# Convolution read straight from the accumulation bank, and the second norm with its projections as a chain of their own

## The chip, the cores and the metric

The kernel runs on one core of one Trainium2 chip. The metric is the device time of one execution in microseconds (us); lower is better. All of the work sits in one launch: five engines (TensorE, here PE; VectorE, DVE; ScalarE, ACT; GpSimd, POOL; and SyncE, SP, which only issues transfers) each run a program of their own and meet at semaphores.

## The reference, cut to what matters

The model is a two-layer decoder over 64 sequences of 128 tokens with 256 features. The change touches only the first layer, whose three sublayers are, for each sequence:

```
x = x + mamba(layernorm(x))            # in_proj, causal conv of 4 taps, scan over time, gate by silu(z), out_proj
x = x + cross_attention(layernorm(x), ctx, ctx, mask)    # q from x, k and v from ctx, 16 heads of 16
x = x + moe(layernorm(x))              # shared expert + top 2 of 16 experts

xc = conv(x_ssm, conv_w, padding=(3, 0)) + conv_b        # per channel: 4 taps over time
x_ssm = silu(xc)
y = scan(dt, A, B, C, x_ssm) + D * x_ssm
y = rmsnorm(y) * silu(z)
```

The routed experts and the second layer come in later phases of the same launch and are the same in both kernels.

## The kernel before

The launch has three phases. Phase 1 does the first layer's three sublayers for all 64 sequences, except for the routed experts, whose rows it scatters; phase 2 runs the experts; phase 3 does the second layer. One sequence fills the 128 partitions with its 128 tokens (or, transposed, with 128 features).

Phase 1 is a software pipeline. The work on a sequence is cut into chains, named by a letter: M (first norm, the step sizes dt and their running sums), V (input projections, convolution, gate), N (scan as masked products, output projection, residual x1), Y (keys and values from the context), X (cross-attention), F (third norm, router, shared expert). Body n of the loop runs M and V for sequence n, N for n-1, Y and X for n-2 and F for n-3. `program` unrolls the first and last bodies, which hold fewer chains, and loops over the full ones. Each chain is a Python generator that yields a step's name before it issues the step, and `weave` runs the generators in the order of the table `ORDER`, one line for each engine. So `Vcv` is step "cv" of chain V, and what stands in the table is the very order in each engine's queue. Every engine takes its queue strictly in order; `done` waits for a signal of this sequence, `was` waits until the previous sequence no longer needs a buffer. Nearly all buffers exist once.

The steps that the text below speaks of:

- POOL: `d0` to `d3` (differences of running sums, L618), `m3` (a mask product, L622), M's `sp` (the softplus series, 13 small operations, L594 to L610), `yg` (gate product, L625), `rms`, `ln1` to `ln3` (four tiny operations each, L582 to L585), F's `sc` (two indirect scatters).
- DVE: `cv` to `cv3` (the convolution: four taps, each in four pieces of 128x128; the first at L817, the others at L819), `m0` to `m2` of N (mask products, L847), `y0` and `y1` (L852), `xs2` (L826), `xdt` (L836, L837), `gz` (L841), `cb` (L830), `x1` (L861), `m0` to `m3` of X (row maxima of scores, L769 and L772), `ho` (heads out, L784 to the second residual at L880), F's `r`, `top` and `slot` (router, L889 to L912), `xo` (L920).
- PE: `bc`, `ip1`, `z` (input projections), `CB`, `xsT`, `v0` to `v3` (scan products, L1488), `yT`, `pr` (output projection), Y's `cT`, `k`, `v`; X's `ln2n`, `q`, `s0`, `s2` (scores), `t0` to `t3` (transposes of probabilities, L1425), `pv` (L1434), `OT`; F's `r`, `rk`, `gu`, `hT`, `dn`.
- ACT: copies out of the banks, `g`/`e` (absolute value and exponential), the softmax, `cth` and `tz` (tanh), `xp`.

The accumulation banks (PSUM) are Q[0] to Q[7]. Q[1] holds in turn, for chain V, `bc`, `ip1`, `CB`, `xsT` and `z`. In the kernel before, ACT's `xp` copies `ip1` to the padded SBUF tile `xpad`, and the convolution reads that.

Of the kernel before, what the change touches and what calls it, by code (L numbers as in the profile page):

```python
# [89 lines left out]
def two_layers(nc, x_d, ctx_d, m0_d, m1_d, w_in, conv_w, conv_b, a_log, d_p, dt_bias, norm_w, w_out,  # L90
# [8 lines left out]
    with ExitStack() as ctx:  # L99
# [105 lines left out]
        xpad = part(IC * (T + NCONV - 1)).rearrange("p (c t) -> p c t", c=IC)  # L205
# [73 lines left out]
        signals("V", "DVE", "conv xs2 cbm xdt gz")  # L279
        signals("V", "PE", "bc ip1 CB xsT z")  # L280
        signals("V", "ACT", "bcT xpad conv_th tz")
# [3 lines left out]
        signals("Y", "DVE", "k0c")  # L285
        signals("Y", "PE", "ctxTps k0 v0")
        signals("Y", "ACT", "ctxT v0c")
        signals("X", "DVE", "ln2_var S0max:4 x2")
        signals("X", "PE", "ln2_Tps q0 S0:4 PT0ps:4 PV0:2")
        signals("X", "ACT", "ln2_xn mrow ln2_T q0c P0:4 PT0s:4 OT0")  # L290
        signals("X", "POOL", "x1r ln2_rstd")
# [30 lines left out]
        links = {"M_DVE": 3, "V_DVE": 3, "X_DVE": 5, "F_DVE": 15, "A_DVE": 5, "C_DVE": 1, "K_DVE": 2, "T_DVE": 7, "M_POOL": 13, "N_POOL": 1, "X_POOL": 3,  # L322
# [71 lines left out]
        def _(sp):  # L394
# [74 lines left out]
            program(sp, "SP", 1, (("M", M, 0), ("N", N, 1), ("Y", Y, 2), ("X", X, 2), ("F", F, 3)))  # L469
# [61 lines left out]
        def _(pool):  # L531
# [6 lines left out]
            g.memset(xpad, 0.0)  # L538
# [92 lines left out]
            def X(b):  # L631
# [5 lines left out]
                centre("ln2", mvX, b, "X_POOL")  # L637
# [11 lines left out]
            program(pool, "POOL", 1, (("M", M, 0), ("N", N, 1), ("X", X, 2), ("F", F, 3)))  # L649
# [68 lines left out]
        def _(dve):  # L718
# [1102 lines left out]
```

How the kernel before makes its waits and increments, by code:

```python
        def done(eng, name, b, k=1):  # L124
            eng.wait_ge(SEM[name], at(name, b, k))
# [1 line left out]
        def was(eng, name, b, k=1):  # L127
            if not isinstance(b, int) or b > 0:
                eng.wait_ge(SEM[name], at(name, b, k) - PER[name])
# [202 lines left out]
        def link(eng, name, b, ins, bare=False):  # L333
            steps[name] += 1
            assert steps[name] <= links[name], name
            ins.then_inc(SEM[f"link_{name}"], 1)
            eng.wait_ge(SEM[f"link_{name}"], at(f"link_{name}", b, steps[name]))
            if bare:
                eng.sem_inc(SEM[f"passed_{eng.engine.name}"], 1)
# [28 lines left out]
        def met(eng, me, k):  # L369
            eng.sem_inc(SEM[f"phase_{me}"], 1)
            for other in ("PE", "DVE", "ACT", "POOL"):
                if other != me:
                    eng.wait_ge(SEM[f"phase_{other}"], k)
# [18 lines left out]
        @block.sync  # L393
# [67 lines left out]
            def F(b):  # L461
                yield "m"
                done(sp, "slot", b)
                tell(sp.dma_start(rows(slot_d, b), meta[:, :]), "meta_out", 16)
                yield "o"
                done(sp, "xo", b)
                tell(sp.dma_start(rows(x2_d, b), xo), "xo_out", 16)
            program(sp, "SP", 1, (("M", M, 0), ("N", N, 1), ("Y", Y, 2), ("X", X, 2), ("F", F, 3)))
            sp.wait_ge(SEM["plan"], 1)
            sp.dma_start(routed_d[SPARE:SPARE + P, :], zero).then_inc(SEM["tails"], 16)
            zeros_behind(sp, range(NE // 2))
            sp.wait_ge(SEM["scattered"], at("scattered", NB, 0))
```

## Time and profile before

| | |
|---|---|
| median of 3 runs | 4827.91 us (4826.06 to 4829.62) |
| the profiled execution | 4827.89 us, its span 4826.3 us |
| PE busy | 4224.3 us, 88% of the span |
| DVE, ACT, POOL busy | 3368.1 us (70%), 2909.1 us (60%), 2734.9 us (57%) |
| mean granted clock of TensorE | 0.923 of full speed |

A busy time is the sum of an engine's instructions over the span. Phase 1 takes about the first 2516 us of it. In phase 1 no engine is busy all the time, so the busy shares do not say what bounds it; the order of the queues and the waits between them do.

### The profile page before, as it was taken

The page shows a single profiled execution, that of the slowest core. Times are in us where ns is not written, and L with a number is a line of the kernel's source. Part 1 is how long each engine was busy: PE and PEld are TensorE (multiplying, and loading weights), DVE is VectorE, ACT ScalarE, POOL GpSimd, SP SyncE. Part 2 cuts the span into 40 slices and gives each one's busy share as a digit, 9 for nine tenths or more (in the row PEclk, how much of TensorE's full clock was granted, in tenths as well). Part 3 has the DMA queues.
Part 4 walks back from the last instruction along what each step waited for, and adds up shares of the span by engine and source line. Part 5 has one row for each costly group of instructions (what it writes and reads, how often), then busy time and mean ns, then how long its engine had stood idle before and what let it go on. Part 6 is the DMA issues. An engine that isn't in the chain of part 4 may idle for free.

```text
span 4826.3 us, 119218 instructions
## 1 busy us (share of the span) xinstructions
PE 4224.3 (88%) x33430; PEld 3093.7 (64%) x33431; DVE 3368.1 (70%) x8668; ACT 2909.1 (60%) x7030; POOL 2734.9 (57%) x4093
## 2 busy tenths in 40 slices
PE   3788888888888888888869979999999999999998
PEld 2666666666666666666647756666666666666665
DVE  2776677666776667766745547777777777777776
ACT  2666666666666666666634436666666666666564
POOL 3666666666666666666622235555555555555554
PEclk9888888888888888888979989999999999999998
DMA  5222222222222222222214411111111111111110
GB/s 155 72 82 90 74 74 74 89 83 74 74 78 92 75 74 74 83 88 75 74 59 145 144 39 31 30 31 31 31 29 31 30 31 31 31 31 31 31 31 18
DMA packets 215885, 304.09 MB, mean 63 GB/s; under 512 B 56608, under 2 KB 167456, under 8 KB 215840
## 3 DMA queue, kind: packets, MB, share of 16 engines
q1 hardware_dynamic: 188864, 240.33, 16.0%
q0 software_dynamic: 19200, 52.45, 3.3%
q10 hardware_dynamic: 7776, 10.75, 0.7%
q8 instruction: 23, 0.38, 0.0%
q14 instruction: 22, 0.18, 0.0%
HBM read 239.19 MB, written 64.23 MB: 63 GB/s over the span
## 4 chain that ended last, share of the span: by engine, by line
PE 51%; POOL 20%; issue 17%; DVE 6%; ACT 2%; POOLq 1%; SPq 1%; DMA 0%; DVEq 0%; ACTq 0%
PE Q L1397 14%; PE Q L1402 8%; POOL arena L618 7%; PE Q L1390 6%; PE Q L1488 4%; PE Q L1425 3%; PE Q L1735 3%; PE Q L1768 3%; PE Q L1589 3%; PE Q L1434 2%; POOL arena L625 2%; PE Q L1601 2%; POOL arena L605 1%; PE Q L1419 1%; POOL arena L606 1%
## 5 line engine op out<-in xcount | busy, mean ns | idle before, releaser
L1402 PE MATMUL Q<-ident,arena 128*128 128x128 f32 x4768 | 801.5, 291 | 148.7 <-ACT arena L1145 35.3
L1402 PEld LDWEIGHTS Q<-ident,arena 128*128 128x128 f32 x4768 | 557.0, 145 | 388.2 <-issue 123.7
L1397 PE MATMUL Q<-Wkvl,arena 128*128 128x512 f32 x1024 | 500.3, 601 | 0.0
L618 POOL TENSOR_TENSOR arena<-arena 128x1024 f32<-128x1024 f32 x256 | 479.4, 1889 | 7.2 <-DMA arena<-cum_rows 7.2
L682 POOL TENSOR_TENSOR l<-l,half_pow 128x8 f32<-128x8 f32 x192 | 318.5, 1659 | 233.2 <-DVE l L1025 231.3
L707 POOL TENSOR_TENSOR arena<-arena,part_of 128x512 f32<-128x512 f32 x256 | 263.7, 1041 | 190.8 <-DVE part_of L1063 190.4
L1488 PE MATMUL Q<-arena 128*16 128x128 f32 x4096 | 223.6, 339 | 169.1 <-DVE arena L847 167.9
L769 DVE TENSOR_REDUCE mx<-Q 128x4 f32<-128x512 f32 x512 | 343.9, 681 | 10.2 <-PE Q L1419 5.5
L1425 PEld LDWEIGHTS Q<-ident,arena 128*128 128x128 f32 x2048 | 244.2, 148 | 116.5 <-issue 84.9
L1425 PE MATMUL Q<-ident,arena 128*128 128x128 f32 x2048 | 314.0, 288 | 1.3 <-ACT arena L1155 0.4
L1155 ACT ACTIVATE arena<-Q,mx 128x128 f32<-128x128 f32 x1024 | 281.8, 372 | 0.7 <-DVE mx L769 0.5
L1419 PE MATMUL Q<-arena 32*128 32x128 f32 x4096 | 278.7, 274 | 0.0
L1162 ACT ACTIVATE arena<-Q 128x512 f32<-128x512 f32 x384 | 222.0, 597 | 83.2 <-PE Q L1425 79.1
L1488 PEld LDWEIGHTS Q<-arena 128*16 128x16 f32 x4096 | 129.4, 107 | 222.2 <-DVE arena L847 169.0
L1202 ACT ACTIVATE arena<-arena 128x1024 f32<-128x1024 f32 x256 | 268.4, 1048 | 0.1
L1199 ACT ACTIVATE arena<-arena 128x1024 f32<-128x1024 f32 x256 | 268.3, 1048 | 0.0
L1419 PEld LDWEIGHTS Q<-arena 32*128 32x128 f32 x4096 | 261.4, 188 | 3.6
L1361 ACT ACTIVATE arena<-Q,mxl 128x256 f32<-128x256 f32 x512 | 235.4, 472 | 45.0 <-DVE mxl L1058 37.6
L1390 PEld LDWEIGHTS Q<-arena,Win 128*128 128x128 f32 x1536 | 235.8, 235 | 33.5 <-issue 29.2
L1434 PE MATMUL Q<-arena 128*17 128x128 f32 x4096 | 208.1, 276 | 41.4 <-ACT arena L1162 41.4
L1390 PE MATMUL Q<-arena,Win 128*128 128x128 f32 x1536 | 236.9, 315 | 3.1 <-ACT arena L1184 2.2
L1397 PEld LDWEIGHTS Q<-Wkvl,arena 128*128 128x128 f32 x1024 | 170.3, 191 | 104.2 <-issue 104.0
(310 smaller groups left out, 10753.3 us busy)
## 6 DMA issues: line engine op xcount, KB each, us to landing
arena<-cum_rows SPq DMA_DIRECT2D x256, 512.0 KB, 6.1
arena<-routed_rows SPq DMA_DIRECT2D x144, 128.0 KB, 2.1
expert_rows<-arena POOLq DMA_DIRECT2D x144, 128.0 KB, 2.0
arena<-in_x_dram SPq DMA_DIRECT2D x128, 128.0 KB, 4.4
arena<-in_ctx_dram SPq DMA_DIRECT2D x128, 128.0 KB
x_rows<-arena SPq DMA_DIRECT2D x128, 128.0 KB, 1.7
arena<-x_rows SPq DMA_DIRECT2D x128, 128.0 KB, 2.3
out_dram<-arena SPq DMA_DIRECT2D x64, 128.0 KB, 1.7
```

The source lines that it names most:

```text
L618: tell(g.tensor_tensor(E8[j], E8[j], cums[:, 8 * j:8 * j + 8].unsqueeze(2).broadcast_to([P, 8, T]), ALU.subtract), "diff")
L682: link(pool, c, b, g.tensor_tensor(l2[:, k, :], l2[:, k, :], half_pow[:, :], ALU.pow), bare=True)
L769: largest = v.tensor_reduce(mx[:, 4 * j:4 * j + 4], pj, AX.X, ALU.max, negate=True)
L1155: last = s_.activation(S[:, j, g, :], banks[j][:, g * T:(g + 1) * T], ACT.Exp, bias=mx[:, 4 * j + g:4 * j + g + 1])
L1202: tell(s_.activation(Ew[j], Ew[j], ACT.Exp, scale=-1.0), "E")
L1390: last = mm(out, lhs(c), rhs(c), start=c == 0, stop=c == n - 1)
L1397: last = mm(out, lhs(c), rhs(c), start=c == 0, stop=c == n - 1)
L1402: last = nc.tensor.transpose(out[:, c * P:(c + 1) * P], src[:, c * P:(c + 1) * P], ident[:, :])
L1419: last = mm(banks[j][:, g * T:(g + 1) * T], QT[r, g, :], KT[r, g // 2, :], start=False, stop=g == NG - 1)
L1425: last = nc.tensor.transpose(bank[:, g * T:(g + 1) * T], S[:, j, g, :], ident[:, :])
L1434: last = mm(bank[32 * (h % 4):32 * (h % 4) + AW + 1, h // 4 * T:(h // 4 + 1) * T], V[:, h, :], PT[:, j, g, :], start=True, stop=True)
L1488: last = mm(Q[3 + j // 2][32 * (i % 4):32 * (i % 4) + HP, (h // 4 % 4) * T:(h // 4 % 4 + 1) * T], xdt[:, h * HP:(h + 1) * HP], E8[j][:, i, :],
```

## The change

- The convolution reads the bank Q[1] directly, tap by tap, with the time shift in the slices instead of in a padded tile. The first tap becomes a multiply-add with two scalars per partition (`tensor_scalar`), the other three stay as they were, with the bank as their source. `xpad`, its memset and ACT's copy `xp` go away. `CB` can no longer use Q[1] beside the convolution, so `CB` and `cb` move behind `z` and `gz`.
- The second norm, its transposes and the query projection move from chain X to chain Y (and from banks Q[5], Q[6] to Q[2]). Y now stands for sequence n-2, X for n-3 and F for n-4: five sequences in flight, 68 bodies instead of 67.
- Chain N swaps the banks of `yT` and `pr`.
- The table `ORDER` for phase 1 is rewritten on all five engines.

```diff
     1: {
         "SP": """
-            Ncb0 Ncb1 Ncb2 Yc Xm Mx Ncb3 Nx Mco Fm Fo
+            Ncb0 Ncb1 Xm Ncb2 Ncb3 Nx Mx Yc Fm Mco Fo
         "POOL": """
-            Nd0 Nd1 Nd2 Xx1r Fln3 Xln2 Mln1 Nd3 Msp Nm3 Fsc Nyg Nrms
+            Nd0 Nd1 Nd2 Fln3 Nd3 Mln1 Fsc Nm3 Msp Yx1r Yln2 Nyg Nrms
...
             def V(b):
                 J = lambda ins, bare=False: link(dve, "V_DVE", b, ins, bare)
-                yield "cv"
-                done(dve, "xpad", b)
-                for k in range(NCONV):
-                    if k:
-                        yield f"cv{k}"
+
+                for late in range(NCONV):
+                    yield f"cv{late}"
+                    if late == 0:
+                        done(dve, "ip1", b)
                     for c in range(IC):
-                        src, wk = xpad[:, c, k:k + T], convw[:, c, k:k + 1]
-                        out = xc[:, c * T:(c + 1) * T]
-                        if k == 0:
-                            last = v.scalar_tensor_tensor(out, src, wk, convb[:, c:c + 1].broadcast_to([P, T]), ALU.mult, ALU.add)
+                        src, wk = Q[1][:, c * T:(c + 1) * T - late], convw[:, c, NCONV - 1 - late:NCONV - late]
+                        out = xc[:, c * T + late:(c + 1) * T]
+                        if late == 0:
+                            last = v.tensor_scalar(out, src, wk, convb[:, c:c + 1], ALU.mult, ALU.add)
                         else:
                             last = v.scalar_tensor_tensor(out, src, wk, out, ALU.mult, ALU.add)
...
-                yield "xp"
-                done(act, "ip1", b)
-                tell(s_.activation(xpad[:, :, NCONV - 1:], cut(Q[1][:, :], IC), ACT.Copy), "xpad")
...
-            program(pe, "PE", 1, (("M", M, 0), ("V", V, 0), ("N", N, 1), ("Y", Y, 2), ("X", X, 2), ("F", F, 3)))
+            program(pe, "PE", 1, (("M", M, 0), ("V", V, 0), ("N", N, 1), ("Y", Y, 2), ("X", X, 3), ("F", F, 4)))
```

The first place is DVE in the middle and second half of a full body. In the rows a line number is that of the kernel they belong to, and rows that only set registers are left out. Before:

```order
L847 TENSOR_TENSOR arena<-arena 128x1024
L769 TENSOR_REDUCE mx<-Q 128x4
L920 TENSOR_TENSOR arena<-Q,arena 128x256
L817 SCALAR_TENSOR_TENSOR arena<-arena,convw,convb 128x128 x4
L819 SCALAR_TENSOR_TENSOR arena<-arena,convw 128x128 x12
L852 TENSOR_TENSOR arena<-Q,arena 128x256
L826 SCALAR_TENSOR_TENSOR arena<-arena 128x512
```

In the changed kernel the same place reads:

```order
L815 TENSOR_SCALAR arena<-Q,convw,convb 128x128 x4
L817 SCALAR_TENSOR_TENSOR arena<-Q,convw,arena 128x127 x4
L817 SCALAR_TENSOR_TENSOR arena<-Q,convw,arena 128x126 x4
L920 TENSOR_TENSOR arena<-Q,arena 128x256
L782 RECIPROCAL rc<-Q 128x16
L783 TENSOR_TENSOR arena<-Q,rc 128x256
L880 TENSOR_TENSOR arena<-arena 128x256
L817 SCALAR_TENSOR_TENSOR arena<-Q,convw,arena 128x125 x4
L852 TENSOR_TENSOR arena<-Q,arena 128x256
L824 SCALAR_TENSOR_TENSOR arena<-arena 128x512
```

The convolution's source is now Q, and `xo` (L920) and `ho` (L782 to L880) stand between its third and its last tap; before, `ho` stood at the start of the body, behind `x1`.

The second place is PE at the end of a full body, behind the transposes of y. Before:

```order
L1434 MATMUL Q<-arena 17x128 x8
L1402 MATMUL Q<-ident,arena 128x128 x4
L1434 MATMUL Q<-arena 17x128 x4
L1397 MATMUL Q<-Win,arena 128x512 x2
L1397 MATMUL Q<-Wout,arena 128x256 x4
```

And in the changed kernel:

```order
L1388 MATMUL Q<-arena,Wq 128x128 x4
L1400 MATMUL Q<-ident,arena 128x128 x4
L1395 MATMUL Q<-Win,arena 128x512
L1400 MATMUL Q<-ident,arena 128x128 x2
L1395 MATMUL Q<-Win,arena 128x512
L1388 MATMUL Q<-arena,Wk 128x128 x4
L1388 MATMUL Q<-Wv,arena 128x256 x2
L1471 MATMUL Q<-arena 128x128
L1395 MATMUL Q<-Wout,arena 128x256 x4
```

Now the query, key and value projections (Wq, Wk, Wv) and `CB` (L1471) stand around `z` (Win) and ahead of the output projection (Wout); `pv` (17x128) has moved to the middle of the body.

The third place is DVE at the start of a full body of the changed kernel, up to the router's maximum:

```order
L752 BN_STATS stF<-arena 128x6
L767 TENSOR_REDUCE mx<-Q 128x4
L770 TENSOR_TENSOR arena<-Q,mx 128x512
L752 BN_STATS stM<-arena 128x6
L752 BN_STATS stX<-arena 128x6
L847 TENSOR_TENSOR arena<-arena 128x1024
L889 TENSOR_REDUCE rt<-Q 128x1
```

Two pairs of L767 and L770 and two L847 stand there. Before, the scores stood behind the router.

## Rows read from the trace of the kernel before

**Rows 1.** Timeline of POOL: start, length, the gate product in three bodies

```profile
105.25 1.27 POOL L625 TENSOR_TENSOR arena<-arena 128x512 f32<-128x512 f32 x1 [3.97 <-DVE arena L852]
211.17 1.28 POOL L625 TENSOR_TENSOR arena<-arena 128x512 f32<-128x512 f32 x1 [3.25 <-DVE arena L852]
...
2425.67 1.27 POOL L625 TENSOR_TENSOR arena<-arena 128x512 f32<-128x512 f32 x1 [3.15 <-DVE arena L852]
```

**Rows 2.** Stretches of phase 1: from:to, length, busy (instructions) of each engine, clock, DMA

```profile
800.00:1100.00 300.00, 249.80 (x2064) 190.25 (x2062) 208.69 (x561) 196.42 (x424) 191.00 (x289) 0.87 0.24 79
...
1011.60:1018.60 7.00, 6.71 (x28) 6.14 (x29) 2.73 (x16) 3.72 (x11) 3.39 (x7) 0.52 0.00 0
```

**Rows 3.** Waits over 40 bodies (500 to 2000 us): total, times, longest

```profile
POOL arena L594 <- DVE arena L804: 244.7, 40, 6.1
...
PE Q L1488 <- DVE arena L847: 105.3, 40, 2.6
```

**Rows 4.** Timeline of one body, DVE: start, length, instruction

```profile
1006.66 0.25 DVE L784 RECIPROCAL rc<-Q 128x16 f32<-128x16 f32 x1
1008.15 0.43 DVE L754 BATCH_NORM_STATS2 stF<-arena 128x6 f32<-128x256 f32 x1
1009.57 1.22 DVE L847 TENSOR_TENSOR arena<-arena 128x1024 f32<-128x1024 f32 x1
1010.72 0.42 DVE L754 BATCH_NORM_STATS2 stM<-arena 128x6 f32<-128x256 f32 x1
1014.97 0.17 DVE L889 TENSOR_REDUCE rt<-Q 128x1 f32<-128x16 f32 x1 [3.50 <-PE Q L1390]
1018.25 0.17 DVE L902 TENSOR_TENSOR selb<-sel 128x16 bf16<-128x16 f32 x1
1021.26 0.68 DVE L769 TENSOR_REDUCE mx<-Q 128x4 f32<-128x512 f32 x1
1022.58 0.68 DVE L769 TENSOR_REDUCE mx<-Q 128x4 f32<-128x512 f32 x1
1028.55 3.24 DVE L817 SCALAR_TENSOR_TENSOR arena<-arena,convw,convb 128x128 f32<-128x128 f32 x4
1031.83 3.56 DVE L819 SCALAR_TENSOR_TENSOR arena<-arena,convw 128x128 f32<-128x128 f32 x12
```

**Rows 5.** Timeline of PE in the same body, and two rows of the last bodies

```profile
1004.05 1.89 PE L1397 MATMUL Q<-Wout,arena 128*128 128x256 f32 x8
1017.41 1.65 PE L1390 MATMUL Q<-arena,Win 128*128 128x128 f32 x8
1020.65 1.98 PE L1397 MATMUL Q<-Wsgu,arena 128*128 128x512 f32 x4
1022.47 1.95 PE L1390 MATMUL Q<-arena,Win 128*128 128x128 f32 x16
2479.09 3.78 PE L1397 MATMUL Q<-Wsgu,arena 128*128 128x512 f32 x4
2491.74 1.76 PE L1434 MATMUL Q<-arena 128*17 128x128 f32 x32
```

**Rows 6.** Single lines: count, shortest/median/longest in ns, first and last start

```profile
L817 DVE SCALAR_TENSOR_TENSOR arena<-arena,convw,convb x256: 332/340/2459, 65.6 to 2419.9; 128x128 f32<-128x128 f32 x128
L622 POOL TENSOR_TENSOR arena<-arena x64: 2361/2409/2424, 98.9 to 2453.0; 128x1024 f32<-128x1024 f32 x64
```

**Rows 7.** Timeline of DVE in the last two bodies: second residual and x2 out

```profile
2466.09 0.48 DVE L861 SCALAR_TENSOR_TENSOR arena<-Q,ss,arena 128x256 f32<-128x256 f32 x1 [5.83 <-PE Q L1397]
2495.70 0.42 DVE L880 TENSOR_TENSOR arena<-arena 128x256 f32<-128x256 f32 x1
2513.48 0.42 DVE L920 TENSOR_TENSOR arena<-Q,arena 128x256 f32<-128x256 f32 x1 [2.14 <-PE Q L1390]
```

**Rows 8.** Timeline of SP and POOL in the second body: a transfer and its user

```profile
69.33 0.36 SPq L437 DMA_DIRECT2D cum_rows<-arena  x1
...
74.90 5.60 POOL L618 TENSOR_TENSOR arena<-arena 128x1024 f32<-128x1024 f32 x3 [7.23 <-DMA arena<-cum_rows]
```

More of the change, by code:

```diff
@@ L278, in two_layers @@
         signals("M", "POOL", "ln1_rstd a")
-        signals("V", "DVE", "conv xs2 cbm xdt gz")
-        signals("V", "PE", "bc ip1 CB xsT z")
-        signals("V", "ACT", "bcT xpad conv_th tz")
+        signals("V", "DVE", "conv xs2 xdt gz cbm")
+        signals("V", "PE", "bc ip1 xsT z CB")
+        signals("V", "ACT", "bcT conv_th tz")
         signals("N", "DVE", "M:3 y2 x1")
@@ L284, in two_layers @@
             sig(n, k)
[L285 to L291, printed above, removed]
+        signals("Y", "DVE", "ln2_var k0c")
+        signals("Y", "PE", "ln2_Tps q0 ctxTps k0 v0")
+        signals("Y", "ACT", "ln2_xn ln2_T q0c ctxT v0c")
+        signals("Y", "POOL", "x1r ln2_rstd")
+        signals("X", "DVE", "S0max:4 x2")
+        signals("X", "PE", "S0:4 PT0ps:4 PV0:2")
+        signals("X", "ACT", "mrow P0:4 PT0s:4 OT0")
         signals("F", "DVE", "ln3_var rmax sel slot hh xo")
@@ L841, in V @@
                 tell(v.scalar_tensor_tensor(gz, tz, 1.0, Q[1][:, :], ALU.add, ALU.mult), "gz")
+                yield "cb"
+                done(dve, "CB", b)
+                was(dve, "M3", b)
+                tell(v.tensor_tensor(cbm, Q[1][:, 0:T], triu[:, :], ALU.mult), "cbm")
             def N(b):
@@ L1213, in N @@
                 done(act, "yTps", b)
-                tell(s_.activation(yT, cut(Q[4][:, :], IC), ACT.Copy), "yT")
+                tell(s_.activation(yT, cut(Q[3][:, :], IC), ACT.Copy), "yT")
             def Y(b):
+                yield "ln2"
+                normal("ln2", x1, xn2, mvX, b)
+                yield "ln2n"
+                copyT("ln2", Q[2], xT2, b)
+                yield "q"
+                done(act, "q0", b)
+                was(act, "S0", b, 4)
+                src = cut(Q[2][:, D:2 * D], DC)
+                dst = QT0.rearrange("p (c k) q -> p c k q", k=2)
+                for k in range(2):
+                    for c in range(DC):
+                        last = s_.activation(dst[:, c, k, :], src[:, c, :], ACT.Identity, bias=bq0s[:, c, k:k + 1], scale=par[:, k:k + 1])
+                tell(last, "q0c")
                 yield "cT"
@@ L1232, in X @@
                 tell(s_.activation(mrow[:, :], mask0i[:, :], ACT.Identity, bias=eps[:, 2:3]), "mrow")
-                yield "ln2n"
-                copyT("ln2", Q[6], xT2, b)
-                yield "q"
-                done(act, "q0", b)
-                src = cut(Q[5][:, 0:D], DC)
-                dst = QT0.rearrange("p (c k) q -> p c k q", k=2)
-                for k in range(2):
-                    for c in range(DC):
-                        last = s_.activation(dst[:, c, k, :], src[:, c, :], ACT.Identity, bias=bq0s[:, c, k:k + 1], scale=par[:, k:k + 1])
-                tell(last, "q0c")
                 yield from softmax(b, banks, S0, mx0, 0)
@@ L1452, in V @@
                 done(pe, "ln1_T", b)
-                was(pe, "gz", b)
+                was(pe, "cbm", b)
                 for k in range(2):
@@ L1474, in V @@
                 tell(last, "z")
+                yield "CB"
+                done(pe, "gz", b)
+                tell(mm(Q[1][:, 0:T], bcT[:, 0, :], bcT[:, 1, :], start=True, stop=True), "CB")
             def N(b):
```

71 lines of the change are left out of this document (32 added, 39 removed).

## The prediction

> **What bounds the kernel now.** I read the page's busy shares (which name no bound), then the stretches, the timeline of one body, the waits and the chain of waits. Phase 1 is a loop: POOL's gate product starts at 211.17 us in one body and at 2425.67 us 59 bodies later [rows 1], so a full body takes 37.53 us, and 64 sequences make about half of the time. In a steady stretch of 300 us no engine is full: PE 250, DVE 209, ACT 196 and POOL 191 us [rows 2]. That is 31.2, 26.1, 24.6 and 23.9 us of a body. So the body is as long as the chain of hand-offs that runs once round it through queues that are taken strictly in order. The waits say the same: POOL stands 6.1 us in each body for DVE's dt ratio and 3.2 us for `y1` [rows 1], PE 2.6 us for the first mask product [rows 3], DVE 3.5 us for the router's product [rows 4].
>
> Two more things lengthen a body. First, PE's clock: from 1011.6 to 1018.6 us the granted clock was 0.52, its lower level of 1.2 GHz, behind the stretch in which PE stood idle for 2.6 us [rows 2, 3]. Four matmuls of an input projection took 1.65 us there, where eight took 1.95 us at the full 2.4 GHz; two products 512 wide took 3.78 us at the low and 1.98 us at the full level [rows 5]. Second, DVE and POOL get in each other's way. The first tap of the convolution takes 0.34 us at the median, but at the most 2.46, and in each body four pieces take 3.24 us [rows 4, 6]: one of them stands for as long as POOL's mask product, 2.41 us [rows 6]. The Trainium skill, page "SBUF — State Buffer", section "Who interferes with whom", says that a VectorE instruction with two SBUF inputs and GpSimd's reads exclude each other for the whole instruction. The trace agrees: the blocked piece has the padded tile and the broadcast bias as its inputs. By that rule the new first tap, whose one tensor lies in a bank, is never blocked; if the pair of engines were in each other's way whatever the operands, the three early taps would last 2.1 us longer and outlast their cover (below) by 0.7 us, and the sum would be 4837 us.
>
> **The change part by part.**
>
> *The convolution.* The first tap now has one input, in the bank, and the others one in the bank and one in SBUF. Nothing here can be blocked by POOL like the piece of 2.46 us: the first tap's four pieces should take about 4 times 0.29, 1.15 us, as four pieces of the later taps do (12 in 3.5) [rows 4]. DVE saves 2.1 us of a body, POOL nothing. ACT saves `xp`, a copy of a full bank (about 0.6 us, as the other copies of a bank), which is not on the path. Does the bank as a source cost time? A 128x256 sum took 0.42 us with both inputs in SBUF and 0.42 us with one in a bank [rows 7], so I take nothing; the bound upward is one piece's 0.05 us, 0.8 us a body. The Trainium skill, "VectorE: DVE Perf Modes", section "Rules for kernel authors", says to copy a bank to SBUF first when many operations will read it, which speaks against this change. By that rule the copy would pay only where an instruction has a faster mode from SBUF, and the two rows show none for a form with two inputs.
>
> *The order.* I followed the new queues once round, from the end of `y1` on DVE to the same point in the next body, always taking the later of "engine free" and "input there". Durations are distances between starts in the timeline of one body; steps under 1 us that have no row of their own are read there too. The path that I find:
>
> - `y1` to `x1`: POOL's gate product 1.27 plus a hand-off 0.08; transposes 0.6; first half of `z` 0.9; context transposes 0.35; second half 0.9 (two such products 1.98 [rows 5]); key and value projections 0.95 and 0.85 (from eight matmuls in 1.95, full clock); `CB` 0.2; `pr` 1.89 [rows 5]; `x1` 0.48 and 0.3 for its waits. Sum 8.8 us. Query, key and value used to run at the low clock beside other work; here they are on the path but at full clock.
> - DVE alone: three norms' moments at 0.71 (two in 1.42), two score steps at 1.32, two mask products at 1.15 [rows 4]: 7.1 us. None of it is new work; it now lies in one queue between `x1` and the router.
> - router's maximum to `sel`: 3.45 [rows 4], plus 0.1 for a hand-off: 3.55 us.
> - PE: rank 0.2, `t0` 0.5, `bc` 1.5 at low clock, `gu` 3.2 (between 1.98 and 3.78, nearer to the low clock), `ip1` 1.95 [rows 5]: 7.35 us.
> - `hT` 0.4, `t1` 0.6, its copy on ACT 0.6, `t3` 0.5, four `pv` steps 1.8 (1.76 [rows 5]), `dn` 0.85, `OT` 0.65, with 0.1 for hand-offs: 5.5 us.
> - `ho` 1.45 (L784 to the next norm at 1008.15 [rows 4]), `cv3` 1.15, tanh 0.7, `xs2` 0.65, `y1` 0.4: 4.35 us.
>
> The sum is 36.65, with 0.05 left over in rounding 36.7 us, 0.83 us less than 37.53. What lies beside it: the first three taps (3.5 us) end 1.4 us before `dn`, so most of what DVE saves there stays hidden; if PE's part between were shorter, it would come out. POOL does its scatters, `m3` and the softplus one after another behind `slot` and ends them about 0.8 us before PE comes to `Mcum`. If that cover goes, each us there lengthens the body. The transfer of the sums now starts some 2.7 us before `y1` ends and took 5.6 us to its user [rows 8], so `d0` starts 3 us after `y1`, 1 us after `rms` lets it. POOL's three differences end at 8.7, the third norm's moments come at 9.5: hidden by 0.8. Behind POOL's late norm wait ACT's `Fln3` and PE's router, which is where a late transfer would come out.
>
> *The extra body.* 68 bodies instead of 67. The last body with F alone took 17.8 us, from the second residual to `xo`, the one with Y, X and F 29.6 [rows 7]. The new one has X and F: between the two, and I take 22. The early bodies get lighter, since X and F start later; today three early bodies take 35.3 us each (105.25 to 211.17 us) [rows 1], 6.6 us less in all, and one more such step may save between 1 and 8 us; I take 5. Together +17 us, between +10 and +28.
>
> *The sum.* 60 full bodies at -0.83 are -50 us, the extra body +17. From the profiled execution's 4827.9 us (span 4826.3 and 1.6 around it; the median of three runs is 4827.91, the same): **4795 us**.
>
> **The rivals.**
>
> *Slower: the low clock lasts longer.* Between the scores at the start and `sel` I find PE busy for some 4 of 10 us, with one gap of 2.3 us and three over 1. Today 7.0 us at the low level follow one gap of 2.6 us [rows 2, 3]. It has to come back during `gu` for my sum. If it comes back only within `ip1`, that costs up to 1.45 us more (3.4 instead of 1.95), and `gu` 0.5 more [rows 5]. The change loses as soon as a body is 0.55 us longer than my sum: 60 bodies must save at least the 17 us of the extra one, 0.28 each, and they save 0.83. At +1.3, a body of 38.0, the time is 4827.9 + 28 + 17 = 4873 us; with all of `ip1` slow (+2) it is 4915. For it speaks that `bc` and `gu` follow directly on the thin stretch; against, that PE is packed from `sel` on.
>
> *Faster: the clock holds.* The gaps are each shorter than today's. Then `bc` saves 0.55 and `gu` 1.4: a body of 34.75 and 4678 us. Against it speaks how little PE does in that stretch.
>
> *Faster: the convolution's 2.1 us come out in full*, since DVE is what is waited for in the second half: 60 times 2.1 is 126, plus 17: 4719 us. For it: the convolution stands between `ip1` and `y0` in the chain of today. Against it: my layout hides it behind `pv` and `dn`.
>
> *No change:* the path is the same length with other names, a body of 37.1 to 37.4, and 4819 to 4837 us.
>
> **How the numbers follow.** My forecast, 4770 to 4817 us: 0.35. Slower by the clock: 0.31. Faster by the clock 0.08, by the convolution 0.14. No change 0.12. Faster by over 0.2% (10 us, about what a measurement of this kernel can tell from no change) is 0.35 + 0.08 + 0.14 = 0.57, same 0.12, slower 0.31. The range reaches down past the convolution's case, to 4705, and up to 4880, past the middle of the slow case; it leaves out the far end of the slow case and the held clock, about 2 in 10.
>
> **What would show it.** In the changed kernel's profile: gate products 36.7 us apart; all 16 pieces of the convolution at about 0.35 us with no long one; the granted clock about 0.85 in the loop, low from before the router until within `gu`; DVE without a gap from `x1` to the router's maximum; POOL idle some 6 us before the scatters. My sum is wrong if `ip1` shows the low clock (slower), if DVE waits long before `xo` and `ho` (then the convolution is hidden, as I say) or does not wait there at all (then it counts), or if POOL's `d0` waits for the transfer well past 3 us after `y1`.

## The result, and the profile after

The changed kernel takes 4860.7 us, the median of 4 runs (4859.21 to 4863.27), beside 4826.99 us for the kernel before. The ratio is 1.0073, with a 95% interval of 1.0055 to 1.009: it is slower by 34 us, where 4795 us and a gain were forecast. The profiled execution took 4860.3 us, its span 4858.7 us.

Timeline of POOL in the changed kernel, the gate product in four bodies (start, length, instruction, idle time before it and what ended that):

```profile
100.98 1.27 POOL L623 TENSOR_TENSOR arena<-arena 128x512 f32<-128x512 f32 x1 [4.76 <-DVE arena L852]
207.33 1.27 POOL L623 TENSOR_TENSOR arena<-arena 128x512 f32<-128x512 f32 x1 [1.75 <-DVE arena L852]
2425.09 1.27 POOL L623 TENSOR_TENSOR arena<-arena 128x512 f32<-128x512 f32 x1 [2.16 <-DVE arena L852]
2460.29 1.27 POOL L623 TENSOR_TENSOR arena<-arena 128x512 f32<-128x512 f32 x1
```

Between the second and the third row lie 59 bodies: 37.59 us each, beside 37.53 before [rows 1] (one of them takes 41.4 us, the others average 37.5). The loop gained nothing, where 0.83 us a body were forecast. It did not lose the 34 us either: the gate product at 2425.09 stands where that of before stood (2425.67 us). Almost all of the loss is behind it.

Timeline of DVE behind the loop: the last residual x1 (L861), xo (L920) and x2 (L880) of the last bodies, and the first instruction of phase 2 (L943):

```profile
2469.51 0.48 DVE L861 SCALAR_TENSOR_TENSOR arena<-Q,ss,arena 128x256 f32<-128x256 f32 x1 [1.30 <-PE Q L1395]
...
2491.93 0.42 DVE L880 TENSOR_TENSOR arena<-arena 128x256 f32<-128x256 f32 x1
...
2529.57 0.43 DVE L880 TENSOR_TENSOR arena<-arena 128x256 f32<-128x256 f32 x1
...
2548.90 0.42 DVE L920 TENSOR_TENSOR arena<-Q,arena 128x256 f32<-128x256 f32 x1 [3.33 <-PE Q L1388]
2551.37 0.27 DVE L943 MEMSET arena<- 128x256 f32 x1 [2.04 <-DMA x_rows<-arena]
```

From the last x1 to the last xo it is 79.4 us, in three bodies of 22.4, 37.6 and 19.3. Before it was 47.4 us, in two of 29.6 and 17.8 [rows 7]. That is 32 us, the whole loss within 2. (From the gate product at 2425.09 to the last x1 it is 4.0 us more than before; the start of phase 1 is 3.8 us shorter and the later phases are 3 us shorter.) So two things have to be explained: why a body is not shorter, and why the last ones are so long.

Stretches of the changed kernel (from:to, length, busy time of PE, weight load, DVE, ACT, POOL, granted clock, DMA), the second one the 14 us behind PE's longest wait in a body:

```profile
800.00:1100.00 300.00, 258.04 (x2062) 191.13 (x2054) 193.84 (x560) 193.23 (x416) 183.49 (x288) 0.82 0.24 79
893.80:907.80 14.00, 13.32 (x81) 9.34 (x82) 10.33 (x35) 9.24 (x20) 6.55 (x8) 0.51 0.08 25
```

DVE is busy for 15 us less of 300 [rows 2]: the convolution's saving is real. POOL is busy for 7.5 less, but that is the order's work: with the new convolution in the old order (`conv_alone` below) the same stretch has DVE at 194.59 and POOL still at 191.05 us. The clock went from 0.87 to 0.82. It now stays at its lower level of 1.2 GHz for 14 us at a time, where it was 7.0. It did not double a body's time at that level, though: before, most bodies had a second low stretch of 3.4 us, which the prediction did not read (granted 0.51 from 841.1 to 844.5 us and 0.50 from 861.6 to 868.4). As a share of time it went from about a quarter to about a third (worked out from 0.87 and 0.82, with 0.5 for the lower level).

The waits over 40 bodies (500 to 2000 us; total, times, longest):

```profile
POOL routed_rows L644 <- DVE meta L912: 267.9, 40, 6.7
...
PE Q L1400 <- ACT arena L1145: 162.6, 116, 2.9
...
POOL arena L633 <- DVE arena L880: 39.1, 36, 1.2
```

POOL stands 6.7 us before the scatters, as forecast. In the last row POOL's `x1r` (L633) waits for x2 (L880), about 1 us a body. The wait itself is not new. The kernel before has it too:

```profile
POOL arena L635 <- DVE arena L880: 27.9, 40, 0.7
```

But there it held up nothing: in one body of that kernel `x1r` runs from 857.86 to 858.59 us, and the moments of the second norm (`mvX`) are ready only at 859.38. In the body of the changed kernel below they are ready at 821.19 us, 20 us before POOL comes to them. What is new is that `x1r` has a finished norm behind it. The price shows in one full body, on POOL, ACT and PE:

```profile
839.84 0.25 POOL L608 TENSOR_TENSOR arena<-arena,Aneg 128x32 f32<-128x32 f32 x1 [0.18 <-POOL arena L607]
840.15 0.41 PE L1444 MATMUL Q<-arena,triu 128*128 128x32 f32 x2
841.15 0.73 POOL L633 TENSOR_TENSOR arena<-arena,bv0b 128x256 f32<-128x256 f32 x1 [1.05 <-DVE arena L880]
841.83 0.19 POOL L580 TENSOR_TENSOR mvX<-mvX,eps 128x1 f32<-128x1 f32 x1
...
843.76 0.60 ACT L1145 ACTIVATE arena<-arena,mvX 128x256 f32<-128x256 f32 x1 [0.86 <-POOL mvX L583]
...
844.41 0.87 PE L1400 MATMUL Q<-ident,arena 128*128 128x128 f32 x6 [1.31 <-ACT arena L1145]
845.32 1.16 PE L1388 MATMUL Q<-arena,Wq 128*128 128x128 f32 x8
846.32 0.60 PE L1400 MATMUL Q<-ident,arena 128*128 128x128 f32 x4
```

The second norm's four tiny operations (L580 to L583) stand behind `x1r` in POOL's queue. So the norm comes late, PE stands 1.31 us at its transposes, and behind them in PE's queue are the query projection (Wq), `yT`, `z` and the output projection, that is x1. The gate product ends at 845.36 us (844.09 and 1.27), but its transposes `yT` start only at 846.32, behind the query projection.

### The profile page after: what moved, and what is told of

Its sections match the earlier page's. It is cut to its first block, busy times and chain, and to the rows that moved or that the text cites. A ratio compares the mean times of both kernels' runs of the same rounds, so it can differ in the third digit from the quotient of the medians.

```text
span 4858.7 us, 118978 instructions
## 1 busy us (share of the span) xinstructions
PE 4291.8 (88%) x33430; PEld 3114.9 (64%) x33431; DVE 3260.6 (67%) x8668; ACT 2883.9 (59%) x6966; POOL 2670.3 (55%) x4092
## 4 chain that ended last, share of the span: by engine, by line
PE 68%; DVE 10%; issue 9%; POOL 5%; ACT 5%; DMA 1%; DVEq 1%; SPq 1%; POOLq 0%; ACTq 0%
PE Q L1395 20%; PE Q L1388 14%; PE Q L1400 11%; PE Q L1423 4%; PE Q L1432 3%; PE Q L1735 3%; PE Q L1768 3%; PE Q L1589 3%; DVE mx L767 2%; ACT arena L1225 2%; PE Q L1601 2%; PE Q L1417 1%; ACT arena L1145 1%; DVE arena L847 1%; PE Q L1487 1%
## 5 line engine op out<-in xcount | busy, mean ns | idle before, releaser
L1400 PEld LDWEIGHTS Q<-ident,arena 128*128 128x128 f32 x4768 | 561.0, 147 | 661.3 <-ACT arena L1145 299.8
L644 POOL DMA_INDIRECT routed_rows<-arena,meta x128 | 150.7, 1178 | 461.8 <-DVE meta L912 439.1
L767 DVE TENSOR_REDUCE mx<-Q 128x4 f32<-128x512 f32 x512 | 350.1, 684 | 9.0 <-PE Q L1417 4.3
L1417 PE MATMUL Q<-arena 32*128 32x128 f32 x4096 | 331.9, 309 | 0.0
L1423 PE MATMUL Q<-ident,arena 128*128 128x128 f32 x2048 | 313.3, 295 | 17.8 <-ACT arena L1162 16.0
L1417 PEld LDWEIGHTS Q<-arena 32*128 32x128 f32 x4096 | 315.0, 221 | 7.2
L1423 PEld LDWEIGHTS Q<-ident,arena 128*128 128x128 f32 x2048 | 251.8, 151 | 100.5 <-issue 66.0
L1388 PEld LDWEIGHTS Q<-arena,Win 128*128 128x128 f32 x1536 | 246.3, 243 | 46.0 <-issue 43.1
L1388 PE MATMUL Q<-arena,Win 128*128 128x128 f32 x1536 | 247.1, 323 | 1.9 <-ACT arena L1184 1.9
L847 DVE TENSOR_TENSOR arena<-arena 128x1024 f32<-128x1024 f32 x192 | 229.6, 1223 | 1.9 <-issue 0.4
```

Source lines behind the costliest of these rows:

```text
L767: largest = v.tensor_reduce(mx[:, 4 * j:4 * j + 4], pj, AX.X, ALU.max, negate=True)
L847: tell(v.tensor_tensor(E8[j], E8[j], cbm.unsqueeze(1).broadcast_to([P, 8, T]), ALU.mult), "M")
L1388: last = mm(out, lhs(c), rhs(c), start=c == 0, stop=c == n - 1)
L1400: last = nc.tensor.transpose(out[:, c * P:(c + 1) * P], src[:, c * P:(c + 1) * P], ident[:, :])
L1417: last = mm(banks[j][:, g * T:(g + 1) * T], QT[r, g, :], KT[r, g // 2, :], start=False, stop=g == NG - 1)
L1423: last = nc.tensor.transpose(bank[:, g * T:(g + 1) * T], S[:, j, g, :], ident[:, :])
```

## The experiments

The theory after the result: `x1r` of a sequence waits for x2 of the one before, now made in the same body; that delays the second norm a little in every body and a lot in the last ones. The rival: the longer low clock eats the loop's gain. A second rival: the convolution's place. Each kernel was timed beside the kernel before on the same chip. Ratios are to that kernel, intervals 95%. Not all kernels had the same chip, so differences between two experiments are given by their ratios, too. Of a queue the diffs show the part that changes, "..." stands for the rest.

**The convolution alone.** Kernel `conv_alone`: the kernel before with the new convolution and `CB` behind `gz`, everything else in its old order.

```diff
-... Fxo Vcv Vcv1 Vcv2 Vcv3 Ny0 Vxs2 Ny1 Vcb Vxdt Vgz Nx1 Xho
+... Fxo Vcv0 Vcv1 Vcv2 Vcv3 Ny0 Vxs2 Ny1 Vxdt Vgz Vcb Nx1 Xho
```

> The kernel before with the convolution alone changed: it reads the bank, the copy to the padded tile is gone, CB and cb stand behind z and gz; chains, stages and the rest of the order as before. Theory A (the gain of the convolution is real and was lost to the order, the clock and the extra body): DVE is on the path from ip1 to y1 there, the blocked piece of 2.46 us goes, and a body gets 1.2 to 2.1 us shorter: 4700 to 4755 us. Rival B (the convolution brings nothing wherever it stands): within 10 us of 4827. Rival C (the bank held longer costs, since CB now waits for gz): slower, over 4840.

4832.43 us, ratio 1.0015 (1.0006 to 1.0024). Timeline of DVE at the place of [rows 4]:

```profile
1029.00 1.35 DVE L815 TENSOR_SCALAR arena<-Q,convw,convb 128x128 f32<-128x128 f32 x4
1030.39 3.42 DVE L817 SCALAR_TENSOR_TENSOR arena<-Q,convw,arena 128x127 f32<-128x127 f32 x12
1035.05 0.42 DVE L852 TENSOR_TENSOR arena<-Q,arena 128x256 f32<-128x256 f32 x1 [1.25 <-PE Q L1399]
1036.90 0.69 DVE L824 SCALAR_TENSOR_TENSOR arena<-arena 128x512 f32<-128x512 f32 x1 [1.42 <-ACT arena L1187]
```

The gain expected under theory A (4700 to 4755 us) did not come. The convolution takes 4.8 us instead of 6.8, and DVE then waits 1.25 us for PE, where it did not wait before, and 1.42 us for the tanh, where it was 0.36 to 0.50. Even in the old order its 2 us were not on the path: the rival by which they come out in full is refuted there. The edit moves `CB`, too, so a small gain of the one and a small loss of the other are not told apart. The granted clock in the stretch from 800 to 1100 us rose to 0.94, from 0.87, and brought nothing either.

**The convolution made dearer.** Kernel `conv_twice`: the changed kernel with the first tap computed twice.

> The changed kernel with the convolution's first tap computed twice (four more pieces of 128x128, 1.4 us of DVE a body). The prediction put the first three taps beside pv and dn with 1.4 us to spare; the profile after shows DVE waiting 0.7 us between the third tap and xo. If the first three taps are hidden, the body grows by only what exceeds that spare, 0.7 us at most: 4860 to 4905 us. If DVE's convolution lies on the path, it grows by the whole 1.4 us: 4945 us or so.

4867.12 us, ratio 1.0071 (1.0057 to 1.0085), against 1.0073 for the changed kernel. 1.4 us more of DVE for each sequence, some 88 us in all, cost about 6 us by the medians and nothing by the ratios. The first three taps are hidden, as the prediction's layout had it. In the loop DVE no longer waits for PE before `xo`, where it waited 0.7 us in the changed kernel, so this cover, forecast at 1.4 us, is used up.

**The bias as a tensor.** Kernel `bias_tensor`:

```diff
-v.tensor_scalar(out, src, wk, convb[:, c:c + 1], ALU.mult, ALU.add)
+v.scalar_tensor_tensor(out, src, wk, convb[:, c:c + 1].broadcast_to([P, T]), ALU.mult, ALU.add)
```

> The changed kernel with the first tap as the two-operand form it had before, source in the bank and the broadcast bias from SBUF, so that one operand more comes from SBUF. If only two inputs in SBUF get in POOL's way, no piece of the first tap is long: all near 0.34 us and the time is that of the changed kernel within 0.2%. If POOL's traffic blocks any instruction that reads a tensor from SBUF twice over its output, some pieces last over 1 us while POOL's mask product runs.

4861.95 us, ratio 1.007 (1.0055 to 1.0085). Single lines (count, shortest/median/longest in ns), first of this kernel, then of the changed one:

```profile
L815 DVE SCALAR_TENSOR_TENSOR arena<-Q,convw,convb x256: 339/343/353, 64.2 to 2415.5; 128x128 f32<-128x128 f32 x128
```

```profile
L815 DVE TENSOR_SCALAR arena<-Q,convw,convb x256: 401/404/414, 64.2 to 2414.7; 128x128 f32<-128x128 f32 x128
```

The very form that stood for up to 2459 ns before [rows 6] is never blocked once its source is a bank. All 256 pieces ran beside some instruction of POOL, but only 25 of them beside its mask product. `conv_alone` makes this firm: 316 pieces of its later taps, with one input in the bank and one in SBUF, ran beside the mask product, and the longest took 352 ns. What blocked the first tap was the second input from SBUF. The Trainium skill, "SBUF — State Buffer", section "Who interferes with whom", states that a VectorE instruction with at most one input in SBUF, outside the modes that use both ports, does not contend with GpSimd; the trace agrees in all of these pieces.

**The second norm ahead of x1r.** Kernel `norm_first`:

```diff
-... Fsc Nm3 Msp Yx1r Yln2 Nyg Nrms
+... Fsc Nm3 Msp Yln2 Yx1r Nyg Nrms
```

> The changed kernel with one swap on GpSimd: the second norm's scale ahead of x1r, so that it no longer waits for the previous sequence's second residual. Theory A (x1r's wait for x2 holds back the whole query and key chain): in the last bodies the chain starts 2 to 13 us earlier, and in a full body 0.3 to 1.0 us comes off: 4790 to 4840 us. Rival B (the wait is covered in full bodies): only the last bodies gain, 4850 to 4858.

4839.73 us, ratio 1.0025 (1.0015 to 1.0035): 21 us below the changed kernel. Bodies of 36.7 and of 37.5 us alternate in stretches (the profiled execution, 4821.86 us, was the fastest of nine). Gate product and x1 in a short body:

```profile
870.17 1.27 POOL L623 TENSOR_TENSOR arena<-arena 128x512 f32<-128x512 f32 x1 [2.05 <-DVE arena L852]
...
878.57 0.48 DVE L861 SCALAR_TENSOR_TENSOR arena<-Q,ss,arena 128x256 f32<-128x256 f32 x1 [1.49 <-PE Q L1395]
```

From the start of the gate product to the end of x1 it is 8.9 us, where three of four bodies of the changed kernel take 9.9: the 1.0 us by which the short bodies are shorter. The wait for x2 is part of the loss, in the loop and behind it. But PE now stands before the running sums for POOL's softplus series: 48.0 us in the 40 bodies from 500 to 2000 us, against 7.7 in the changed kernel.

**Filler matmuls.** `fill_before` puts 12 small matmuls of the identity, into columns that nobody reads, ahead of `v0` in the kernel before. `fill_after` puts 25 a body into the changed kernel, where PE stands idle between the scores and `sel`.

> The kernel before with 12 such extra matmuls a body ahead of the first scan product, where TensorE stands idle for 2.6 us. If the low clock of 7.0 us a body costs there too: a body gets 1 to 1.7 us shorter, 4725 to 4770 us. If its projections there are hidden behind DVE's router: within 15 us of 4827.

> The changed kernel with 25 extra small matmuls a body (128x128 by 64 columns, into a free part of bank Q[0]; their results are not used) put where TensorE waits: 12 ahead of the third norm's transposes, 3, 6 and 4 ahead of the router, the first norm's transposes and the ranks. Theory A (the low clock, 14.7 us of a body, costs the time): the granted clock stays at 1.00, gu takes 1.98 us instead of 3.42 and bc 0.95 instead of 1.9, a body gets 1.5 to 2.5 us shorter, 4705 to 4770 us. Rival B (the path there is DVE's and ACT's, the clock only fills waits): 4850 to 4870. Rival C (the extra matmuls stand in the way): slower than 4880.

`fill_before`: 4804.55 us, ratio 0.995 (0.9934 to 0.9967). `fill_after`: 4873.68 us, ratio 1.0097 (1.0079 to 1.0115). Both missed their forecast gains (4725 to 4770 and 4705 to 4770 us). The bodies of `fill_before` are 36.0 us in some stretches and 37.5 in others: in the kernel before, the low clock costs up to 1.5 us a body, not always given back. In `fill_after` the part of the body that ran at 0.51 now runs at the full level, and yet it is no faster (the two intervals overlap; its bodies take 37.55 us). Stretch, then timelines of POOL and PE in the same body (gate product at 811.53, the next at 849.08):

```profile
823.50:837.50 14.00, 13.64 (x135) 11.23 (x133) 11.82 (x39) 11.20 (x26) 6.46 (x8) 1.00 0.06 20
```

```profile
833.53 1.40 POOL L644 DMA_INDIRECT routed_rows<-arena,meta  x1 [6.82 <-DVE meta L912]
835.23 0.96 POOL L644 DMA_INDIRECT routed_rows<-arena,meta  x1 [0.30 <-issue]
836.21 2.38 POOL L620 TENSOR_TENSOR arena<-arena 128x1024 f32<-128x1024 f32 x1
838.54 0.24 POOL L592 TENSOR_TENSOR arena<-arena 128x32 f32<-128x32 f32 x1
...
844.36 0.25 POOL L608 TENSOR_TENSOR arena<-arena,Aneg 128x32 f32<-128x32 f32 x1 [0.18 <-POOL arena L607]
```

```profile
844.67 0.41 PE L1449 MATMUL Q<-arena,triu 128*128 128x32 f32 x2 [2.79 <-POOL arena L608]
```

PE finishes its part early and stands 2.79 us for the end of the softplus series, which on POOL lies behind the scatters and the fourth mask product: 11 us from the first scatter to L608. The sums start 33.1 us behind the gate product. In the body of the changed kernel shown above, the series ended at 840.09 (839.84 + 0.25) and PE, which had just finished its work before them, began the sums at 840.15, 33.7 us behind its gate product at 806.42. That is no chance of this body: in the loop the sums begin 0.05 to 0.18 us behind the end of the series, and in 8 of 54 bodies PE stands 1.9 us for it. So two paths of nearly equal length end there, PE's at the low clock and POOL's. A faster clock alone cannot pay.

**POOL's path.** `sp_first` moves the softplus series ahead of the mask product in the changed kernel; `pool_order` does it in `norm_first`.

```diff
-... Fsc Nm3 Msp ...
+... Fsc Msp Nm3 ...
```

> The changed kernel with one exchange in POOL's queue: the softplus series ahead of the fourth mask product. If POOL's series is one of two paths of equal length at the end of a body, this alone is worth little, since x1r still waits for x2 and the second norm with it: the period 37.0 to 37.5, 4825 to 4860 us. If POOL's queue alone set the end in the changed kernel, it gains as much as it did in pool_order on top of norm_first, 0.9 us a body or more: 4810 us or less.

> norm_first with the softplus series ahead of the fourth mask product on POOL. There PE waited 1.5 us a body for the series before the running sums. If POOL's work behind the router's slot (scatters, mask product, softplus) sets the end of a body, the sums come 2.4 us earlier, the last scan product then waits for the mask product, and a body is 1.0 to 1.6 us shorter: 4740 to 4780 us. If the low clock sets it, the body falls back to 37.5 or 36.7 us all the same and the time is within 10 us of norm_first (4830 to 4845).

`sp_first`: 4848.48 us, ratio 1.0032 (1.002 to 1.0044). `pool_order`: 4769.62 us, ratio 0.9877 (0.9862 to 0.9891), 36.26 us a body. Against the changed kernel the one exchange brings 12 us, the other 21, and both together 91; by the ratios 0.41%, 0.48% and 1.96%. That is how two paths of equal length look: each edit alone shortens only one of them. One rival stays: most bodies of `sp_first` and many of `norm_first` take 37.5 us, a length that bodies of other kernels have as well (see the end), so something else may hold a body there until both edits are made.

**The clock once more, with POOL's path loosened.** `pool_fill` is `pool_order` with the 25 fillers. `m3_dve` is `pool_order` with the fourth mask product on DVE (POOL's queue, then DVE's, in the diff), `m3_fill` is that with the fillers.

```diff
-... Fsc Msp Nm3 Yln2 Yx1r Nyg Nrms
+... Fsc Msp Yln2 Yx1r Nyg Nrms
-... Nm2 Msp Xm3 Fhg ...
+... Nm2 Msp Xm3 Nm3 Fhg ...
```

> pool_order with the 25 filler matmuls a body of fill_after, which held the clock except for some 4 us at the end of a body, where PE stood idle 2.8 us for the softplus series. If the fillers gained nothing in fill_after because the clock's gain was spent waiting for POOL, they gain here: 36 us a body or less, 4745 us or less, and below pool_order. If they gain nothing because they delay what they stand in front of, the time is at or above pool_order's.

> pool_order with the fourth mask product on DVE (1.2 us there, where it waited 1.9 us for the gate's tanh) instead of POOL (2.4 us). In pool_order PE no longer waited for POOL at the end of a body, so if the path there is PE's own part at the low clock, it changes little: 4755 to 4785 us. If POOL still set it, a body is 1 us or more shorter: 4710 us or less.

> m3_dve with the 25 filler matmuls a body. In pool_fill the clock was full, but x2's sum on DVE stood 2.4 us beside POOL's mask product and PE waited 1.55 us for that product. Without the product on POOL both go: if these two ate the clock's gain, a body is 34.3 to 35.5 us, 4660 to 4730 us, and below m3_dve. If the clock is worth nothing at full POOL and DVE load, it comes out at or above m3_dve.

`pool_fill`: 4788.87 us, ratio 0.9918 (0.9905 to 0.9931), slower than `pool_order` with a stretch clock of 0.97. About 6 us of the 19 lie in the first bodies (fourth gate product at 207.87 instead of 202.00 us), the rest in bodies of 36.46 instead of 36.26 us. Its x2 (L880) shows a likely reason, a sum of two tensors in SBUF that took 0.42 us before [rows 7] and 426 ns at the median in `pool_order`. Single lines first, then the timeline of POOL and DVE in one body:

```profile
L880 DVE TENSOR_TENSOR arena<-arena x64: 424/2408/2590, 168.6 to 2459.6; 128x256 f32<-128x256 f32 x64
```

```profile
857.11 2.34 POOL L620 TENSOR_TENSOR arena<-arena 128x1024 f32<-128x1024 f32 x1
...
857.31 2.42 DVE L880 TENSOR_TENSOR arena<-arena 128x256 f32<-128x256 f32 x1 [0.22 <-DVE arena L783]
```

With the series ahead of it and PE earlier, the mask product now falls onto another of DVE's instructions with two inputs in SBUF. `m3_dve`: 4755.14 us, ratio 0.9841 (0.9827 to 0.9854). `m3_fill`: 4740.81 us, ratio 0.9809 (0.9795 to 0.9822), 35.6 us in nearly all bodies, stretch clock 1.00; the forecast had been 34.3 to 35.5 us a body and at most 4730 us. So the clock is worth something once both other paths are out of the way, but only 14 us in all. `m3_fill` is the fastest kernel of the study together with `all_of_it` below.

**The last bodies.** `tail_order` is `norm_first` with an order of its own for the last three bodies, scores and second norm first, the router's chain F last. `tail_router` is the same with F first and the projections in its gaps. `all_of_it` puts the latter into `m3_fill`. PE's queue in the two orders:

```diff
-Xs0 Xs2 Yln2n Yq YcT Yk Yv Fln3n Fr Xt0 Frk Xt1 Fgu Fguh Xt2 Xt3 FhT Xpv Xpv0 Xpv1 Xpv2 Xpv3 Fdn XOT
+Xs0 Fln3n Xs2 Fr Yln2n Yq Frk Xt0 YcT Fgu Fguh Yk FhT Yv Xt1 Fdn Xt2 Xt3 Xpv Xpv0 Xpv1 Xpv2 Xpv3 XOT
```

> The changed kernel with the second norm ahead of x1r on POOL (as in norm_first) and, for the last three bodies only, an order of their own in which scores, second norm, query, key and value projections of chains X and Y stand ahead of the router's chain F on every engine. If the loss of 35 us at the end of phase 1 is the second norm and the projections of the last sequence exposed behind x2 of the sequence before, phase 1 ends about 12 us earlier than in norm_first (second residual of the last sequence to the end of phase 1 some 64 us instead of 76) and the time is 4828 or less; intervals of full bodies stay as in norm_first. If the last bodies cost what they do because an emptied pipeline runs at the low clock whatever the order, phase 1 ends within 3 us of norm_first.

> norm_first with another order for the last three bodies. In tail_order the residual x2 of the last sequence had to wait until the router's chain F of the sequence before had written xo (the buffer of x2 exists once), and F stood last in every queue. Here F stands first on every engine, query, key and value projections in its gaps. If the 79 us from x1 of the last sequence to its xo are a matter of order, the body with X and F shrinks from 37 to 20 us, as I had priced it, and the end of phase 1 comes 10 us or more earlier than in norm_first: 62 to 68 us from x1 to xo instead of 74, 4830 us or less. If they are the latency of two sequences' attention at a low clock one behind the other, x1 to xo stays at 72 us or more.

> m3_fill with the last three bodies of tail_router. By the same reasoning 5 to 12 us below m3_fill if the order of the last bodies counts, the same within 5 us if not.

`tail_order`: 4836.44 us, ratio 1.001 (0.9996 to 1.0024), where 4828 us or less were expected. `tail_router`: 4823.11 us, ratio 1.0 (0.9991 to 1.0009). `all_of_it`: 4742.43 us, ratio 0.9829 (0.9816 to 0.9843), no different from `m3_fill`: its last x1 to its last xo take 68.2 us instead of 75.6, but six bodies of its profiled loop take over 38 us, where `m3_fill` had four. Its forecast gain of 5 to 12 us did not show. Timed, `tail_router` is 0.25% below `norm_first` in ratio; how the time divides is read from the traces. The last x1, the two x2 and the last xo, first of `norm_first`, then of `tail_router`:

```profile
2436.51 0.48 DVE L861 SCALAR_TENSOR_TENSOR arena<-Q,ss,arena 128x256 f32<-128x256 f32 x1 [1.30 <-PE Q L1395]
...
2459.69 0.42 DVE L880 TENSOR_TENSOR arena<-arena 128x256 f32<-128x256 f32 x1
...
2491.14 0.42 DVE L880 TENSOR_TENSOR arena<-arena 128x256 f32<-128x256 f32 x1
...
2510.48 0.42 DVE L920 TENSOR_TENSOR arena<-Q,arena 128x256 f32<-128x256 f32 x1 [3.33 <-PE Q L1388]
```

```profile
2431.75 0.48 DVE L868 SCALAR_TENSOR_TENSOR arena<-Q,ss,arena 128x256 f32<-128x256 f32 x1 [1.30 <-PE Q L1402]
...
2456.25 0.42 DVE L887 TENSOR_TENSOR arena<-arena 128x256 f32<-128x256 f32 x1
...
2480.23 0.43 DVE L887 TENSOR_TENSOR arena<-arena 128x256 f32<-128x256 f32 x1
...
2499.55 0.42 DVE L927 TENSOR_TENSOR arena<-Q,arena 128x256 f32<-128x256 f32 x1 [3.33 <-PE Q L1395]
```

That makes 79.4 us in the changed kernel (22.4 + 37.6 + 19.3), 74.0 in `norm_first` (23.2 + 31.5 + 19.3), 67.8 in `tail_router` (24.5 + 24.0 + 19.3). `tail_order`, expected at some 64, stayed at 79.8: its x2 waited until F, last in the queues, had written xo, since the buffer of x2 exists once. Of the 32 us more than before, 5.4 are the second norm behind `x1r`, some 6 the place of F, and 20 remain for the added body itself.

## Why the prediction was wrong

The profiled time, 4860.3 us, is 65 us above the forecast. 53 of them are the loop, which was to give 50 us and cost 3; some 11 are the extra body, forecast at +17 and measured at +28 (32 behind the loop less 3.8 at the start), at the upper end of its range (+10 to +28); the rest is around the last x1 and in the later phases. Both failures have one step in common: the sum gave no time to `x1r` and to the second norm behind it on POOL.

**The extra body was mis-sized.** The prediction took 22 us for the body with X and F, "between the two" shorter bodies, less 5 at the start, together +17. The start gave back 3.8 us (the fourth gate product at 207.33 instead of 211.17). But behind the loop it was +32. The body with X and F takes 37.6 us, longer than the body with Y, X and F of before, because the second norm and the projections of the last sequence fall into it. The prediction had looked at which chains a body holds, not at what the second norm waits for. `x1r` of a sequence needs x2 of the one before; with X one body later, this x2 is made in the same body. Timeline of POOL and PE in the last body but one of the changed kernel, behind x2 at 2491.93:

```profile
2492.51 0.72 POOL L633 TENSOR_TENSOR arena<-arena,bv0b 128x256 f32<-128x256 f32 x1 [8.43 <-DVE arena L880]
2493.19 0.18 POOL L580 TENSOR_TENSOR mvX<-mvX,eps 128x1 f32<-128x1 f32 x1
...
2496.46 2.07 PE L1388 MATMUL Q<-arena,Wq 128*128 128x128 f32 x8 [0.47 <-ACT arena L1137]
...
2501.35 2.08 PE L1388 MATMUL Q<-arena,Wk 128*128 128x128 f32 x8 [0.47 <-ACT arena L1229]
2503.22 1.91 PE L1388 MATMUL Q<-Wv,arena 128*128 128x256 f32 x4
2506.44 0.39 PE L1526 MATMUL Q<-mrow,mask_w 32*128 32x512 f16 x2 [1.31 <-ACT mrow L1240]
```

POOL waited 8.43 us with a norm whose input lay ready, and only 14 us later come the scores. With both waits ordered away the body takes 24.0 us, so 22 was right for a body of that content and wrong for this queue.

**The loop: the path was longer than the sum by 0.94 us a body.** Its terms against the body from 844.01 to 881.69, the end of `y1` to the end of the next one, 37.7 us: `y1` to x1 took 9.95 instead of 8.8, since the query projection, for which the sum has no term, stood 1.0 us between gate product and `yT`, put there by the wait for x2 shown above; DVE alone 7.2 (7.1 forecast); maximum to `sel` 3.5 (3.55); PE from rank to `ip1` 7.8 (7.35), as `bc` took 1.91 and `gu` 3.20; `hT` to `OT` 4.8 (5.5), where `pv` took 1.29 instead of 1.8; `ho` to `y1` 4.5 (4.35). One body in four is 37.2 us long; there the first term is 9.4. So the failed step is the same as in the last bodies: `x1r` in front of the second norm, on POOL. `norm_first`, without it, has bodies of 36.7 us in its shorter stretches, with 8.9 us for this term. That this is the forecast to the tenth is partly luck: PE's term was 0.45 us too short and the one behind it 0.7 too long. And `norm_first` takes 37.5 us in its other stretches, so this step alone does not bring the forecast gain. The second step is the cover that the prediction gave to POOL's series, 0.8 us, and that is not there (below); with both put right, `pool_order` takes 36.26 us a body.

**The clock rival** came nearest in its number (4873 us), but not by its mechanism. The clock was low for longer than before, and it came back within or just behind `gu`, as the main forecast had said; `ip1` took its 1.95 us. Holding it (`fill_after`) brought nothing.

**Right.** The 16 pieces of the convolution and no long one (335 to 414 ns), its first taps hidden (with 0.7 us to spare, not 1.4), DVE without a gap from x1 to the router's maximum, POOL idle before the scatters for 6.7 us, `d0` 3.4 us behind `y1` (3 forecast). The 0.8 us of cover between POOL's series and PE's sums was not there: the sums began 0.06 us behind the end of the series. This path is part of what kept the clock's gain from coming out; even with it loosened, full clock brought only 14 us (`m3_fill` against `m3_dve`).

## What to carry to other kernels

- When a chain moves to a later body, list for every buffer that exists once who must have finished with it, and in which body that now happens. An operation that waits for it belongs behind everything in its queue that does not.
- Price the last and first bodies by following a sequence through them, not by interpolating between bodies with more and fewer chains. Here 60 bodies with a small gain stood against a tail with a loss that size.
- When an exchange brings little, look for a second path that ends at the same place before giving it up: 12 and 21 us alone were 91 together (0.4%, 0.5% and 2.0% by the ratios).

## What was not expected of the hardware

The low stretches of TensorE's clock do not begin at the same place of each body. In `norm_first` gate products were 36.7 to 37.0 us apart from 833.40 to 980.64. The granted clock falls within these four stretches of 1 us, and from the share of each that was low the falls lie at 845.1, 882.7, 920.2 and 957.8, 37.5 or 37.6 us apart:

```profile
845.00:846.00 1.00, 0.70 (x4) 0.37 (x6) 0.97 (x3) 1.00 (x3) 1.00 (x1) 0.57 0.27 94
882.00:883.00 1.00, 0.81 (x4) 0.51 (x6) 0.91 (x2) 1.00 (x3) 1.00 (x1) 0.84 0.06 19
920.00:921.00 1.00, 1.00 (x16) 1.00 (x13) 0.81 (x4) 1.00 (x2) 0.69 (x4) 0.61 0.00 0
957.00:958.00 1.00, 0.69 (x14) 0.49 (x10) 0.82 (x4) 1.00 (x2) 0.75 (x3) 0.89 0.00 0
```

The next fall is at 991.9, 34 us later. In `pool_order`, with bodies of 36.26 us, four falls read in the same way lie at 866.1, 903.7, 937.8 and 975.4, that is 37.6, 34.1 and 37.6 us apart, on the average about the length of a body.

The kernel before, `fill_before`, `norm_first`, `sp_first` and `fill_after` all have long stretches of bodies of just 37.5 us, though their work differs and `fill_before` falls to 36.0 in between; only `m3_fill`, at full clock, and `all_of_it` have 35.6 nearly throughout. That bodies settle on the distance of the clock's falls is argued from this, not shown; the falls may as well follow the bodies.

In `m3_fill` a low stretch can be priced. Three of its four long bodies (39.6, 39.3 and 38.7 us) hold one each: the granted clock was 0.50 from 648.5 to 658.7, from 1222.0 to 1232.2 and from 1474.6 to 1484.8 us, and 1.00 from 660 to 1220. So 10.2 us at the lower level cost 3.1 to 4.0 us there, fillers included. Why the clock fell in these bodies and not in their neighbours is open.

The first tap with two scalars took 0.404 us from the bank, the form with a tensor as its second operand 0.343.
